# One comparison over four tiles in place of four comparisons: two of the three one-hot tables of a graph network's first edge pass

## The reference, cut to what matters

```python
# layer 0, on every edge, then summed by target node (col = dst)
h = jnp.concatenate([x[row], edge_attr], axis=1)
h = jax.nn.relu(h @ W1a + b1a) @ W1b + b1b
summed = jax.ops.segment_sum(h, col, num_segments=x.shape[0])
cnt = jax.ops.segment_sum(jnp.ones((h.shape[0],), h.dtype), col, num_segments=x.shape[0])
...
# layer 1: out-degree and in-degree, and a sum of gathered rows
deg_out = jnp.clip(jax.ops.segment_sum(ones_e, src, num_segments=N), 1.0)
agg = jax.ops.segment_sum(h[src], dst, num_segments=N)
...
# layer 2: a mean of gathered rows; layer 3: two sums of rows gathered by source node and relation
```

## Time and profile before

| | |
|---|---|
| median of three runs | 4286.95 us (4286.9 to 4287.56) |
| the profiled execution | 4286.95 us, of which 4285.0 us are the span of the profile |
| PE busy over the span | 2873.1 us (67%) |
| POOL busy | 3011.0 us (70%) |
| ACT busy | 1801.4 us (42%) |
| DVE busy | 1494.3 us (35%) |
| pass 0, first to last gather call | 66.4 to 1125.8 us |

### The profile page before, as it was taken

One profiled execution on the slowest core, in us unless ns is written; L12 is line 12 of the kernel. 1 busy time (PEld: TensorE's weight loads), 2 busy tenths in 40 slices (PEclk: granted clock), 3 DMA queues, 4 the chain that ended last, 5 costly groups with the idle time before them and its releaser, 6 DMA issues.

```text
span 4285.0 us, 57007 instructions
## 1 busy us (share of the span) xinstructions
PE 2873.1 (67%) x18556; PEld 2379.5 (56%) x18556; DVE 1494.3 (35%) x5844; ACT 1801.4 (42%) x4884; POOL 3011.0 (70%) x3155
## 2 busy tenths in 40 slices
PE   6999999999889997999944444444443333333333
PEld 5888888888767775666624343434343333333333
DVE  6888888888762225433310000000000000000000
ACT  1444454444341113211155555555545454444543
POOL 4777777777437773777657777777776777777776
PEclk8999999999999997999955555555555555555555
DMA  6776676766647774777622222222221222222222
GB/s 205 212 213 209 212 216 212 213 211 212 192 125 203 202 202 121 218 224 220 173 60 63 68 68 63 62 68 68 63 68 50 55 57 57 55 55 56 57 55 52
DMA packets 413114, 556.61 MB, mean 130 GB/s; under 512 B 67041, under 2 KB 287969, under 8 KB 412545
## 3 DMA queue, kind: packets, MB, share of 16 engines
q0 software_dynamic: 114112, 262.48, 22.6%
q1 hardware_dynamic: 277184, 264.23, 20.5%
q10 hardware_dynamic: 21506, 26.10, 1.8%
HBM read 450.01 MB, written 102.55 MB: 129 GB/s over the span
## 4 chain that ended last, share of the span: by engine, by line
POOL 26%; issue 9%; PE 9%; DMA 6%; ACT 0%; DVE 0%; POOLq 0%; ACTq 0%; DVEq 0%; SPq 0%
POOL work L528 26%; PE bank L1123 8%; DMA work<-table_rel,reli 6%; PE bank L1732 0%; DMA table_rel<-work 0%; ACT work L1744 0%; POOLq L595 0%; ACT work L1804 0%; PE bank L1781 0%; DVE X L1865 0%; POOLq L95 0%; PE bank L1730 0%; ACTq L1808 0%; DVE work L1155 0%; PE bank L2001 0%
## 5 line engine op out<-in xcount | busy, mean ns | idle before, releaser
L528 POOL DMA_INDIRECT work<-table_rel,reli x1664 | 1570.0, 944 | 571.5 <-issue 479.7
L1123 PE MATMUL bank<-work 128*128 128x72 f32 x3328 | 752.7, 419 | 1217.9 <-DMA work<-table_rel,reli 1217.9
L1123 PEld LDWEIGHTS bank<-work 128*128 128x128 f32 x3328 | 710.8, 324 | 1281.1 <-DMA work<-table_rel,reli 1281.1
L528 POOL DMA_INDIRECT work<-table_pre,srci x832 | 807.2, 970 | 270.9 <-issue 268.1
L1108 DVE TENSOR_TENSOR acc<-acc,bank 128x72 f32 x208 | 47.8, 230 | 1982.9 <-PE bank L1123 1982.9
L1910 ACT ACTIVATE work<-iota,local 128x72 f32<-128x72 f32 x1664 | 429.1, 341 | 402.3 <-PE bank L1123 402.3
L1915 ACT ACTIVATE work<-work,ew,src_lo 128x72 f32<-128x72 f32 x1664 | 584.8, 433 | 7.0
L1062 PE MATMUL bank<-work,acc 128*128 128x360 f16 x2574 | 437.8, 316 | 30.3 <-DVE acc L1193 18.0
L764 PE MATMUL bank<-w1a,work 128*128 128x256 f32 x1664 | 442.8, 392 | 19.9 <-DVE work L729 11.1
L528 POOL DMA_INDIRECT work<-table_mean,srci x312 | 303.7, 973 | 168.7 <-issue 88.4
L863 ACT ACTIVATE work<-work 128x512 f32<-128x512 f32 x416 | 252.0, 629 | 361.3 <-DVE work L729 359.6
(11 more groups left out here) (264 smaller groups left out, 3063.5 us busy)
## 6 DMA issues: line engine op xcount, KB each, us to landing
work<-adj SPq DMA_DIRECT2D x104, 720.0 KB
adj<-X SPq DMA_DIRECT2D x130, 450.0 KB
work<-ea_cols SPq DMA_DIRECT2D x208, 256.0 KB
work<-adj SPq DMA_DIRECT2D x52, 810.0 KB
work<-table_rel,reli POOLq DMA_INDIRECT x1664, 2.5
work<-table_pre,srci POOLq DMA_INDIRECT x832
table_rel<-work ACTq DMA_DIRECT2D x25, 512.0 KB
table_rel<-work SPq DMA_DIRECT2D x25, 512.0 KB, 2.9
```

Source lines behind the costliest of these rows:

```text
L528: pool.indirect_dma_start(into[:, u, :], None, tables[p], bass.IndirectOffsetOnAxis(ap=idx_of(p)[:, t:t + 1].bitcast(U32), axis=0)).then_i ...
L1123: mm = pe.matmul(bank[4 + n % LATE_BANKS][:, 0:PAIR_WIN], late_gat[n % LATE][:, u, :], late_hot[:, n % LATE_HOTS, u * PAIR_WIN:(u + 1) * P ...
```

## The change

The four comparisons that make `hot` become one instruction that compares the 64 column numbers, repeated for four tiles, with the four columns of `local`, each repeated 64 times (the helper `one_hot_of`, which is there already). The four comparisons of `hot_hi` become one in the same manner, which reads the f32 table `iota` where the bf16 table `iota_b` was read. `hot_lo` stays as it was.

```diff
         def one_hot(dve, g, n, q):
             dve.wait_ge(seg_done, n + (1 + SLOTS0 - HOTS))
             hq = q % HOTS
-            for u in range(U):
-                dve.tensor_scalar(hot[:, hq, u * WIN:(u + 1) * WIN], iota[:, 0:WIN], local[:, bass.ds(g * U + u, 1)], None,
-                                  ALU.is_equal)
-            for u in range(U):
-                dve.tensor_scalar(hot_hi[:, hq, u, :], iota_b[:, 0:NT], src_hi[:, bass.ds(g * U + u, 1)], None, ALU.is_equal)
+            one_hot_of(dve, g, hot[:, hq, :])
+            dve.tensor_tensor(hot_hi[:, hq, :, :], iota[:, 0:NT].unsqueeze(1).broadcast_to([P, U, NT]),
+                              src_hi[:, bass.ds(g * U, U)].unsqueeze(2).broadcast_to([P, U, NT]), ALU.is_equal)
             for u in range(U):
                 ins = dve.tensor_scalar(hot_lo[:, hq, u, :], iota_b[:, :], src_lo[:, bass.ds(g * U + u, 1)], None,
                                         ALU.is_equal)
```

## The result

The changed kernel took 4306.87 us (median of five runs, 4306.57 to 4311.47), the kernel before 4286.95 us; the ratio is 1.0051, with a 95% interval from 1.0037 to 1.0064. The change makes the kernel slower by 0.5%, some 20 us. The forecast was 4285.9 us, within 0.2% of before, in a range from 4275 to 4298 us.

A forecast was written before the change was run, and what follows sets the result against it. POOL's gather calls were taken to bound pass 0. From 4286.95 us, 9.6 us came off for the removed instructions and 8.5 us was added for the new ones, giving 4285.9 us, in a range from 4275 to 4298 us.

The forecast's parts named there:

- POOL is the bound of pass 0: In pass 0, POOL's 832 gather calls never stand still and set the pace, 5.1 us a group.
- rival 4: In pass 0, VectorE is the bound after all; POOL's floor caps the gain at 4266 us; chance 0.03.
- -9.5 us for L648: In pass 0, removing the four L648 comparisons frees 61 stretched POOL calls of 9.5 us in all.
- +8.5 us: In pass 0, the two new wide instructions stretch POOL's calls by 41 ns a group, over 208 groups.
- rival 3: At gather call starts in pass 0, new instructions stand more often than by chance: +21.2 us, 4298.6 us; chance 0.10.
- I see nothing that ties the one-hots to a fixed place in a call: In pass 0, landings scatter by more than a 1.25 us step, so the measured 25 ns an instruction was taken.

The follow-up runs named there:

- e14: The kernel before without the codes from the third dense group on: 4276.95 us, 15.1 us under the kernel before.
- e11: The changed kernel with each wide comparison cut in two halves: 4322.47 us, 30.4 us over the kernel before.
- e13: The kernel before without the comparisons of hot and hot_hi from the fifth group on: 4289.97 us, 2.1 us under the kernel before.
- e12: The changed kernel with hot's wide comparison between sums and first add, hot_hi's between the two adds: 4299.72 us, 7.6 us over the kernel before.
- e1: The changed kernel with hot_hi back to four instructions, only hot made by one: 4303.0 us, 9.1 us over the kernel before.
- e7: The changed kernel with the four comparisons of hot_lo between the two wide ones: 4304.22 us, 10.3 us over the kernel before.
- e5: The changed kernel with the four comparisons of hot_lo ahead of the two wide ones: 4318.45 us, 24.5 us over the kernel before.
- e6: The changed kernel with hot_lo made by one wide comparison too: 5102.2 us, on a chip where the kernel before took 5113.62 us.
- e8: The kernel before without hot and hot_hi from the fifth group on: 5086.98 us, on a chip where the kernel before took 5113.62 us.
- e10: The changed kernel without the codes from the third dense group on: 5089.64 us, on a chip where the kernel before took 5113.62 us.

## Why the prediction was wrong

**POOL is the bound of pass 0: right.** It waits for next to nothing, before and after, and in the table the change of the excess and the change of the time go together from -19 and -15 us (e14) to +29 and +30 us (e11). VectorE's 146 us less were worth nothing, as said. That is also why rival 4 falls.

**"What counts is its hold on POOL: -9.5 us for L648": wrong, and it is the first step that failed.** Measured by e13 it is nothing (excess 17 against 20 us, a time 2.1 us less, not told from none). I had looked at what VectorE ran near the *end* of a stretched call, and found L648 there 61 times. What stretches a call is what runs 0.13 us after its *start*. In the call at 75.52 that is an instruction of the codes, the middle one of the three that the timeline of the kernel before merges here:

```profile
74.76 1.39 DVE L677 TENSOR_SCALAR X<-X 128x900 bf16<-128x900 f16 x3
75.52 1.09 POOL L528 DMA_INDIRECT work<-table_pre,srci  x1 [0.30 <-issue]
```

It began 0.17 us before the call and ended 0.27 us into it; 0.27 + 0.82 = 1.09 us is the call's length. The L648 four, begun at 0.55 us, were bystanders that the codes always have behind them. The rule for this, end of the holder plus 0.82 us, stood in my own prediction for L640, and I did not try it on the other half of the stretched calls. By it 111 of the 144 stretched calls of the kernel before fall to the codes, with 16.1 us, and six to L648, with 0.3 us. Two more, among them the longest call of 1.88 us, end 0.86 us after a third instruction of the codes and hold 1.9 us. e14 shows the same by taking the codes away. So the rows on L648, which the prediction set beside the Trainium skill's sentence on `tensor_scalar`, do not bear it out; those on the codes do.

**"+8.5 us" for the new instructions: too small, and it is the second step.** As single hits they cost about that (9.4 us in e12, where nothing else can happen). Left out was that a call that waits is not let in at the joint between two instructions that follow at once: from L640 to L648, and from the codes to L640. In passes 1 and 2, from which I took the price, L640 stands alone between sums from PSUM, so the case could not be seen there; I had priced two neighbours as two that stand alone. The 40 calls that were handed on hold 19.8 us, nearly the whole loss, and those held by one wide comparison alone 6.4 us. A call handed on costs up to 0.79 us, more than the 0.29 + 0.23 us a group that rival 3 took for the most. The sum as measured: some 0 for the removal, and +22 us of excess.

That it is the *next* instruction that matters shows best at one and the same place. In the changed kernel 22 calls met an L640 begun 0.142 to 0.157 us before them, and 20 were handed on to the wide comparison behind it. In e1 and e7, where narrow ones stand behind it, 44 calls met it at that place, and none was. The last instruction of the codes, begun 0.138 to 0.149 us before a call, handed on 10 of 11 calls in the changed kernel, where the L640 follows, and none of 10 in the kernel before, where four narrow ones follow.

**"I see nothing that ties the one-hots to a fixed place in a call": wrong as well.** The landings do scatter, but POOL holds VectorE up in turn. In the timeline above the four of L651 take 0.91 to 0.93 us beside the calls at 121.56 and 143.21, and 0.74 us beside the one at 318.95, where nothing is in their way. The fourth is held until late in POOL's call, and what follows it starts at a place fixed to the call. The same calls come again and again: 53 single hits of L648, most of them of 1.00 to 1.01 us like that at 121.56, and the long ones of 1.36 to 1.37 and 1.73 us. This is read from the trace; no kernel here tested it by itself.

Rival 3 had the sign, and a price (4298.6 us) that would have been met at twice the geometric rate. Its mechanism, more hits than by chance, has a small part in it: some 111 calls were held by a wide comparison (18 by L640 alone, 53 by L648 alone, 40 handed on), where chance gives 208 times (0.28 + 0.22) of 1.25, which is 83. That is 1.3 times, short of the 1.7 times from which it was to decide. The time is in the calls that are handed on.

The Trainium skill (SBUF — State Buffer, "Who interferes with whom") says that `tensor_tensor` with both inputs in SBUF contends with GpSimd's reads; its section "Summary: rules for kernel authors" says that the second one to issue is blocked until the first finishes. The runs agree for one instruction (a call of 1.06 us ends 0.82 us after the L640 that it met). They go beyond it for several: the call of 1.73 us waited through three. Its remark that a probe did not see `tensor_tensor` stall a DMA does not hold for the indirect calls here.

No version here beats the kernel before, apart from e14, which leaves the codes out. e12 is the best that keeps both wide comparisons, and it is 0.16% slower than before. What the runs point to is the codes' 15 us, not the one-hots; a form of the codes that holds POOL less was not tried. Nor was a wide comparison that reads its column numbers from PSUM: all eight banks are in use by TensorE during the pass.

## What to carry to other kernels

Before cheaper instructions on an engine that waits anyway, ask what they hold that the engine at the bound needs: here VectorE's work was free in time, and what counted was whether the instruction ran as a GpSimd gather call began. Four narrow `tensor_scalar` were cheaper for POOL (0.3 us in all) than one wide `tensor_tensor` of two SBUF tables (9 us for two of them standing alone, 22 us as neighbours). Where such instructions are needed, do not let one follow another at once: with narrow comparisons between them the loss was halved (e7), with adds that read PSUM it was 7.6 instead of 19.9 us (e12), and cutting them in two made it worse (e11); and when a stretched call is put down to a neighbour, check that its length follows from where that neighbour ends.

## What the runs showed that I had not expected

- A gather call that has to wait can be passed over at the joint between two VectorE instructions with both inputs in SBUF, between the codes' `tensor_scalar` and such an instruction, and now and then between two of the codes: calls of 1.36, 1.46 and 1.73 us in place of 0.945 us. It is not certain each time: at 318.95 the call got in between L640 and L648.
- The place within some 0.02 us goes with it. All 30 calls that the changed kernel's L640 handed on met one begun 0.142 to 0.157 or 0.221 to 0.235 us before them; of the 18 that got in, 16 met one begun elsewhere, as at 318.95 (0.18 us). The last of the codes handed on to the L640 in 10 of the 11 cases in which it was begun 0.141 to 0.147 us before, and in none of the 15 in which it was begun 0.162 to 0.170 us before. In e5 the place made no difference, so it is not the whole rule, and no kernel moved it on purpose.
- Halving such instructions makes it worse (excess 49 against 42 us), since four without a gap mostly hold as one.
- `tensor_scalar` on 64 f32 or 50 bf16 columns costs POOL next to nothing (excess 17 against 20 us when all are gone), but the same operation on 600 or 900 columns, 0.44 us long on the mean, costs 15 us of the kernel's time.
- On one chip the same kernel took 5113.62 us, and in its siblings e6 and e8 to e10 POOL waits some 600 us in all (607 in e8) for something outside its core.
